# A decoder layer with attention, a selective scan and routed adapters: x times sigmoid as one ScalarE function in place of Tanh and a VectorE product

## The chip, the cores and the metric

The kernel runs on one core of one Trainium2 chip, as one launch. The metric is the device time of that launch in microseconds (us); the median of three runs stands for a kernel. Five engines work side by side, each with its own queue in program order: TensorE (PE) for matrix products, VectorE (DVE), ScalarE (ACT), GpSimd (POOL) and SyncE (SP). They meet only at semaphores, and DMA queues move data beside them.

## The reference

Four batches of 512 tokens, width 512, float32. Three blocks, each added to x:

```
x = x + attention(layernorm(x))                 # 16 heads, 2 key/value heads, causal, rotary
x = x + mamba(hidden=ctx, z=layernorm(x))
x = x + ffn(layernorm(x))                       # silu(gate)*up with rank-16 adapters of 8 experts, top 2

mamba:  c  = depthwise causal conv, 4 taps, of (ctx @ in_proj) + conv_b
        u  = silu(c)                            # silu(v) = v * sigmoid(v)
        dt, B, C = split(u @ x_proj);  dt = softplus(dt @ dt_proj + dt_proj_b)
        state = state * exp(dt * A) + dt * u * B      # over 512 steps, 16 states a channel
        y  = sum(state * C) + D * u
        out = y * silu(z)
```

The gate of the convolution is `u = silu(c)`; the gate of z is `y * silu(z)`. The silu of the feed-forward block is not part of the change.

## The kernel before

Work goes batch by batch, with channels or tokens in tiles of 128 partitions (four tiles of 128x512 for every activation). Each engine's program is written out by hand, in the same order of stages. For batch 0 there is a **head**: in-projection, convolution (VectorE), gate, x-projection (TensorE), softplus inputs (ScalarE), and then a polynomial and the scan on VectorE. The **scan** of a batch is 59 pieces of VectorE work (11 for the polynomial, 48 for 16 states) that a fixed table (`PLAN_FIRST`, `PLAN_NEXT`) spreads over slots of the other stages. After the head come the attention projections and 32 attention steps of batch 0.

Then for t = 0, 1, 2 there is a **transition**, the feed-forward stage of batch t, and the attention of batch t+1. The feed-forward stage has 33 evaluations (`evaluate`: ScalarE Silu, then VectorE times `up`), with scan pieces of batch t+1 from the fifth on. Batch 3 has a transition and a feed-forward stage without a next batch beside them.

The transition, in program order. For each of four tiles of tokens i: TensorE projects the attention output (L871), VectorE adds it to x (`first_sum`, L1170) and takes the statistics (`deviation`), GpSimd the power -1/2, VectorE normalizes (`scaled`, L1026) into `hz`, ScalarE gates (`gate_z`, L662) and VectorE multiplies (`gate_y`). `gate_stages` staggers these: at the fourth tile VectorE does its sum and statistics, then `scaled` of tile 2, `gate_y` of tile 1, `scaled` of tile 3, `gate_y` of tile 2, `gate_y` of tile 3. ScalarE does `gate_z` of tiles 0 to 2, then `conv_tap` of one tile (L521, L522: it frees the PSUM bank of that tile of the next in-projection), then `gate_z` of tile 3, then `conv_tap` of the three others. TensorE does three tiles of the next in-projection (`project_in`, L737; the third needs the bank that the first `conv_tap` frees), then the transposes of the gated output (`transpose_gated`, L880) when all four tiles are gated, then the fourth tile. VectorE sums again (`second_sum`, L1189) and normalizes; TensorE transposes, computes the router (L922) and the base product of feed-forward tile 0 (L892, 16 matmuls), while VectorE routes. ScalarE applies Exp to the router's logits (`ffn_masks`, L666), moves masks (L669), does `evaluate(t, 0)`, the convolution's gate of batch t+1 (`conv_gate`), and `split_first`. VectorE does `evaluate(t, 0)`, `activate(t + 1)` and then `mask_low`. TensorE's x-projection `project_x` (L745) waits tile by tile on `u_ready`.

The convolution's weights and bias are halved beforehand (`conv_half`), so `conv_sb` holds c/2, and silu(c) = (tanh(c/2) + 1) * c/2.
Of the kernel before, what the change touches and what calls it, by code (L numbers as in the profile page):

```python
# [7 lines left out]
ALU = mybir.AluOpType  # L8
ACT = mybir.ActivationFunctionType
# [5 lines left out]
NT = L // P  # L15
# [6 lines left out]
JT = DI // P  # L22
# [169 lines left out]
def decoder_layer(nc, x, ctx_t, wq, wk, wv, wo, w_in, w_x, w_dt, w_lora, w_r, b_down, a_down, w_tiles, w_adapt, w_down,  # L192
                  vectors, constants, out, bc_rows):
    with ExitStack() as stack:
        def sb(name, shape, dt=F32):
            return stack.enter_context(nc.sbuf_tensor(name, shape, dt))
# [4 lines left out]
        def sem(name):  # L201
            return stack.enter_context(nc.semaphore(name))
# [39 lines left out]
        hz = r2[:, 0:4, :]  # L242
        silu_z = [r2[:, k, :] for k in (8, 9, 10, 12)]
# [8 lines left out]
        y_sb = sb("y_sb", [P, JT, L])  # L252
# [5 lines left out]
        u_sb, exp_v, relu_v, conv_sb = state[:, 0, :, :], state[:, 1, :, :], decay[:, 0, :, :], decay[:, 1, :, :]  # L258
# [52 lines left out]
        pv_done = sem("pv_done")  # L311
        inv_moved = sem("inv_moved")
        x1_ready = sem("x1_ready")
        tanh_z = sem("tanh_z")
        z_chain = sem("z_chain")
        gated_ready = sem("gated_ready")
        x2_ready = sem("x2_ready")

        tap_ready = sem("tap_ready")
        conv_chain = sem("conv_chain")  # L320
        conv_tanh = sem("conv_tanh")
        u_ready = sem("u_ready")
        xdbl_full = sem("xdbl_full")
        xdt_ready = sem("xdt_ready")
# [187 lines left out]
        def _(act):  # L512
# [13 lines left out]
            def conv_gate(b):  # L526
                for j in range(JT):
                    act.wait_ge(conv_chain, b * 3 * JT + 3 * j + 3)
                    nc.scalar.activation(exp_v[:, j, :], conv_sb[:, j, :], ACT.Tanh).then_inc(conv_tanh, 1)

            def split_first(b):
                act.wait_ge(xdbl_full, b + 1)
# [80 lines left out]
            def attention(b, slots):  # L613
# [43 lines left out]
                for i in range(NT - 1):  # L657
                    gate_z(b, i)

            def gate_z(b, i):  # L660
                act.wait_ge(xn_ready["z"], b * NT + i + 1)
                nc.scalar.activation(silu_z[i], hz[:, i, :], ACT.Tanh, scale=0.5).then_inc(tanh_z, 1)  # L662

            def ffn_masks(t):
                act.wait_ge(router_shift, t + 1)
# [344 lines left out]
        def _(dve):  # L1010
            tt, ts, stt = nc.vector.tensor_tensor, nc.vector.tensor_scalar, nc.vector.scalar_tensor_tensor
# [23 lines left out]
            def convolve(b, tiles):  # L1035

                for j in tiles:
                    bank, count = use(("xin", j), b)
                    dve.wait_ge(tap_ready, b * JT + j + 1)
                    dve.wait_ge(work_free[bank], count + 1)  # L1040
                    for back in range(1, TAPS):
                        tap = conv_half[:, TAPS * j + TAPS - 1 - back:TAPS * j + TAPS - back]
                        stt(conv_sb[:, j, back:L], xin_sb[:, j, 0:L - back], tap, conv_sb[:, j, back:L],
                            ALU.mult, ALU.add).then_inc(conv_chain, 1)
                        dve.wait_ge(conv_chain, (b * JT + j) * 3 + back)

            def activate(b):

                for j in range(JT):
                    dve.wait_ge(conv_tanh, b * JT + j + 1)  # L1050
                    stt(u_sb[:, j, :], exp_v[:, j, :], 1.0, conv_sb[:, j, :], ALU.add, ALU.mult).then_inc(u_ready, 1)

            def scan_piece(b, piece):
                kind, n = piece
                if kind == "poly":

                    if n == 0:
                        dve.wait_ge(softplus_in, b + 1)
                        ts(du_sb[:], exp_v, POLY[-1], None, ALU.mult).then_inc(poly_chain, 1)
                    elif n < NPOLY:  # L1060
                        dve.wait_ge(poly_chain, b * (NPOLY + 2) + n)
                        stt(du_sb[:].rearrange("p j l -> p (j l)"), du_sb[:].rearrange("p j l -> p (j l)"),  # L1062
                            POLY[NPOLY - 1 - n], exp_v.rearrange("p j l -> p (j l)"), ALU.add, ALU.mult)\
                            .then_inc(poly_chain, 1)
                    elif n == NPOLY:
                        dve.wait_ge(poly_chain, b * (NPOLY + 2) + n)
                        tt(dt_sb[:], du_sb[:], relu_v, ALU.add).then_inc(poly_chain, 1)
                    else:
                        dve.wait_ge(poly_chain, b * (NPOLY + 2) + n)
                        tt(du_sb[:], dt_sb[:], u_sb, ALU.mult).then_inc(poly_chain, 1)  # L1070

                        nc.vector.memset(decay[:, :, :, 0:1], 0.0).then_inc(dt_ready, 1)
                    return
                base = b * 3 * NS + 3 * n
                flat = state[:, n % 2, :, :].rearrange("p j l -> p (j l)")
                if kind == "mul":
                    if n == 0:
                        dve.wait_ge(poly_chain, (b + 1) * (NPOLY + 2))
                        dve.wait_ge(y_init, b * JT + JT)
                    elif n >= 2:  # L1080
                        dve.wait_ge(y_added, 16 * (b * NS + n - 1))
                    dve.wait_ge(bc_loaded[n % 2], 16 * (NS // 2) * b + 16 * (n // 2) + 16)
                    row = bc_sb[:, n % 2, 0, :].unsqueeze(1).to_broadcast([P, JT, L])
                    tt(state[:, n % 2, :, :], du_sb[:], row, ALU.mult).then_inc(scan_chain, 1)  # L1084
                elif kind == "run":
                    dve.wait_ge(decay_ready, b * JT * NS + JT * n + JT)
                    dve.wait_ge(dt_ready, b + 1)
                    dve.wait_ge(scan_chain, base + 1)
                    nc.vector.tensor_tensor_scan(flat, decay[:, n % 2, :, :].rearrange("p j l -> p (j l)"), flat, 0.0,  # L1089
                                                 ALU.mult, ALU.add).then_inc(scan_chain, 1)  # L1090
                else:
                    dve.wait_ge(scan_chain, base + 2)
                    row = bc_sb[:, n % 2, 1, :].unsqueeze(1).to_broadcast([P, JT, L])
                    tt(state[:, n % 2, :, :], state[:, n % 2, :, :], row, ALU.mult).then_inc(scan_chain, 1)  # L1094
# [78 lines left out]

            def gate_y(b, j):

                dve.wait_ge(tanh_z, b * NT + j + 1)
                stt(silu_z[j], silu_z[j], 1.0, hz[:, j, :], ALU.add, ALU.mult).then_inc(z_chain, 1)
                if j == 0:
                    dve.wait_ge(y_added, 16 * (b * NS + NS))
                dve.wait_ge(z_chain, b * NT + j + 1)  # L1180
                stt(silu_z[j], y_sb[:, j, :], 0.5, silu_z[j], ALU.mult, ALU.mult).then_inc(gated_ready, 1)

            def second_sum(t):

                for i in range(NT + 1):
                    if i < NT:
                        bank, count = use(("yt", i), t, True)
                        dve.wait_ge(work_full[bank], count + 1)
                        tt(xb[:, i, :], ps_w[:, bank, :], xa[:, i, :], ALU.add).then_inc(work_free[bank], 1)  # L1189
                        dve.wait_ge(work_free[bank], count + 1)  # L1190
                        deviation("ffn", t, xb, i)
                    if i >= 1:
                        scaled("ffn", t, xb, xn, i - 1)

                nc.vector.tensor_copy(scrap[:], vec[0:1, 0:1]).then_inc(x2_ready, 1)
# [86 lines left out]
            ts(decay_rate[:], decay_rate[:], -1.0, None, ALU.mult).then_inc(consts_ready, 1)  # L1282
            dve.wait_ge(conv_halved, 1)
            convolve(0, range(JT))
            activate(0)
            dve.wait_ge(consts_ready, 4)
            dve.wait_ge(loaded["x"], 16)
            normalize("att", 0, xa, xn_att)
# [5 lines left out]
            for t in range(BATCH - 1):  # L1294
                second_sum(t)
                convolve(t + 1, [0])
                route(t)
                convolve(t + 1, range(1, JT))
                evaluate(t, 0)
                activate(t + 1)  # L1300
                mask_low(t)
                for e in range(1, EVALS):
                    evaluate(t, e)
                    if e in NORM_SLOTS:
                        dve.wait_ge(loaded["x"], 16 * t + 32)
                        deviation("att", t + 1, xa, NORM_SLOTS.index(e))
                    for piece in PLAN_NEXT[e]["dve"]:
                        scan_piece(t + 1, piece)
                    if e in NORM_SLOTS:
                        scaled("att", t + 1, xa, xn_att, NORM_SLOTS.index(e))  # L1310
                weigh_down(t)
                for f in range(FT):
                    rotate(t + 1, f)
                    for piece in PLAN_NEXT[DOWN + f]["dve"]:
                        scan_piece(t + 1, piece)
                finish(t)
                attention(t + 1, PLAN_NEXT)
# [104 lines left out]
```

## Time and profile before

| | |
|---|---|
| median of 3 runs | 1612.33 us (1610.44, 1612.33, 1622.39) |
| profiled execution, its time | 1609.58 us |
| its span, first to last instruction | 1607.8 us |
| mean granted TensorE clock | 0.884 |
| PE busy | 1392.1 us (87%) |
| DVE busy | 1129.0 us (70%) |
| ACT busy | 677.2 us (42%), with 56 ACT_TABLE_LOAD |
| POOL busy | 112.0 us (7%) |

A share of busy time is a mean over stages with different limits. 1.8 us of the profiled execution's time lie outside its span. Times in rows are microseconds from the start of the span; "idle before" is how long the engine had nothing to run, with the instruction that ended it.

### The profile page before, as it was taken

The page shows a single profiled execution, that of the slowest core. Times are in us where ns is not written, and L with a number is a line of the kernel's source. Part 1 is how long each engine was busy: PE and PEld are TensorE (multiplying, and loading weights), DVE is VectorE, ACT ScalarE, POOL GpSimd, SP SyncE. Part 2 cuts the span into 40 slices and gives each one's busy share as a digit, 9 for nine tenths or more (in the row PEclk, how much of TensorE's full clock was granted, in tenths as well). Part 3 has the DMA queues.
Part 4 walks back from the last instruction along what each step waited for, and adds up shares of the span by engine and source line. Part 5 has one row for each costly group of instructions (what it writes and reads, how often), then busy time and mean ns, then how long its engine had stood idle before and what let it go on. Part 6 is the DMA issues. An engine that isn't in the chain of part 4 may idle for free.

```text
span 1607.8 us, 16071 instructions
## 1 busy us (share of the span) xinstructions
PE 1392.1 (87%) x5768; PEld 680.2 (42%) x5768; DVE 1129.0 (70%) x1279; ACT 677.2 (42%) x1491; POOL 112.0 (7%) x116
## 2 busy tenths in 40 slices
PE   5756667999998799899999699899989698799999
PEld 2333334444443354434444255444444255454444
DVE  4899997557989775737998866737998967621120
ACT  5155553344543574343552376251562277211110
POOL 0000001000200000000210000100110000100000
PEclk8855558999999699899999678999999869789999
DMA  4166662114667631112766822012566751102113
GB/s 190 40 151 154 141 144 47 41 49 112 169 144 174 166 67 27 40 35 75 181 142 158 197 70 54 27 31 75 144 150 154 168 134 28 27 13 66 49 33 85
DMA packets 53277, 158.80 MB, mean 99 GB/s; under 512 B 5072, under 2 KB 10704, under 8 KB 44752
## 3 DMA queue, kind: packets, MB, share of 16 engines
q0 software_dynamic: 9216, 67.11, 20.3%
q1 hardware_dynamic: 25664, 54.23, 10.2%
q10 hardware_dynamic: 18320, 36.45, 8.5%
q8 instruction: 47, 0.77, 0.2%
q14 instruction: 30, 0.25, 0.0%
HBM read 86.20 MB, written 4.46 MB: 56 GB/s over the span
## 4 chain that ended last, share of the span: by engine, by line
issue 29%; PE 29%; DVE 28%; DMA 6%; ACT 5%; POOL 3%; ACTq 0%; DVEq 0%; POOLq 0%
DVE state L1089 9%; DMA y_sb<-state 6%; PE ps_a L892 5%; PE ps_a L972 4%; DVE state L1084 4%; PE ps_a L818 3%; DVE state L1094 3%; PE ps_w L871 3%; PE ps_a L904 2%; PE ps_b L832 2%; POOL rstd L476 2%; ACT r L624 2%; PE ps_b L912 2%; PE ps_w L780 2%; DVE neg_max L1124 2%
## 5 line engine op out<-in xcount | busy, mean ns | idle before, releaser
L892 PE MATMUL ps_a<-xt,w_sb 128*128 128x512 f32 x704 | 317.5, 605 | 0.0
L1089 DVE TENSOR_TENSOR_SCAN state<-decay,state 128x2048 f32<-128x2048 f32 x64 | 282.8, 4419 | 7.1 <-ACT decay L582 2.9
L1262 DVE TENSOR_TENSOR r<-r,ps_a 128x512 f32<-128x512 f32 x132 | 88.7, 683 | 208.9 <-ACT r L676 208.9
L818 PE MATMUL ps_a<-r 32*128 32x512 f32 (+3 forms) x512 | 140.5, 634 | 83.2 <-ACT r L624 57.8
L892 PEld LDWEIGHTS ps_a<-xt,w_sb 128*128 128x128 f32 x704 | 136.4, 195 | 172.3 <-issue 172.3
L676 ACT ACTIVATE r<-ps_a 128x512 f32<-128x512 f32 x132 | 78.5, 597 | 299.4 <-PE ps_a L904 160.4
L582 ACT ACTIVATE decay<-dt_sb,decay_rate 128x511 f32<-128x511 f32 x256 | 162.9, 711 | 63.2 <-DVE state L1094 31.2
L624 ACT ACTIVATE r<-ps_a,neg_max 128x128 f32<-128x128 f32 (+3 forms) x256 | 133.8, 534 | 117.7 <-DVE neg_max L1124 117.1
L904 PE MATMUL ps_a<-r,wb_sb 128*128 128x512 f32 x352 | 168.4, 601 | 11.1 <-DVE r L1262 8.9
L972 PE MATMUL ps_a<-wd_sb,r 128*128 128x512 f32 x352 | 162.3, 613 | 0.0
L1084 DVE TENSOR_TENSOR state<-du_sb,bc_sb 128x2048 f32<-128x2048 f32 x64 | 146.3, 2287 | 4.5 <-DMA y_sb<-state 4.3
L1094 DVE TENSOR_TENSOR state<-state,bc_sb 128x2048 f32<-128x2048 f32 x64 | 146.0, 2281 | 0.7
L832 PE MATMUL ps_b<-cst,r 128*128 128x128 f32 x640 | 119.6, 329 | 25.4 <-ACT xt L636 16.8
L1124 DVE TENSOR_REDUCE neg_max<-ps_a 128x2 f32<-128x256 f32 (+3 forms) x128 | 104.0, 814 | 21.6 <-PE ps_a L821 20.6
L904 PEld LDWEIGHTS ps_a<-r,wb_sb 128*128 128x128 f32 x352 | 65.4, 191 | 102.4 <-issue 95.7
L486 POOL DMA_DIRECT2D y_sb<-state x64 | 56.1, 877 | 738.7 <-DVE state L1094 654.7
L972 PEld LDWEIGHTS ps_a<-wd_sb,r 128*128 128x128 f32 x352 | 69.8, 199 | 88.0 <-issue 85.4
L832 PEld LDWEIGHTS ps_b<-cst,r 128*128 128x128 f32 x640 | 88.5, 172 | 34.4 <-issue 28.8
L818 PEld LDWEIGHTS ps_a<-r 32*128 32x128 f32 x512 | 50.2, 239 | 119.6 <-ACT r L624 79.6
L476 POOL TENSOR_TENSOR rstd<-var_eps,cst 128x1 f32<-128x1 f32 x48 | 56.0, 1168 | 554.5 <-DVE var_eps L1022 554.5
L912 PE MATMUL ps_b<-r,ad_sb 128*128 128x512 f32 x176 | 87.6, 622 | 1.4 <-DVE r L1262 1.4
L1062 DVE SCALAR_TENSOR_TENSOR du_sb<-du_sb,state 128x2048 f32<-128x2048 f32 x36 | 82.4, 2288 | 0.6
(122 smaller groups left out, 1465.8 us busy)
## 6 DMA issues: line engine op xcount, KB each, us to landing
y_sb<-state POOLq DMA_DIRECT2D x64, 1024.0 KB, 9.7
bc_sb<-bc_rows ACTq DMA_DIRECT2D x64, 512.0 KB, 5.1
w_sb<-in_w_tiles SPq DMA_DIRECT2D x44, 512.0 KB, 3.9
wd_sb<-in_w_down SPq DMA_DIRECT2D x44, 256.0 KB, 3.5
wb_sb<-in_w_adapt SPq DMA_DIRECT2D x44, 128.0 KB, 2.1
xa<-in_x SPq DMA_DIRECT2D x4, 1024.0 KB, 5.1
out_x<-xb SPq DMA_DIRECT2D x16, 256.0 KB, 6.9
xn_att<-in_ctx_t SPq DMA_DIRECT2D x4, 512.0 KB, 6.3
```

Of the source, the lines that this page charges most:

```text
L582: nc.scalar.activation(decay[:, n % 2, j, 1:L], dt_sb[:, j, 1:L], ACT.Exp, scale=decay_rate[:, j, n:n + 1]).then_inc(decay_ready, 1)
L624: nc.scalar.activation(probs[:, (2 * s + k) % 4, 0:(i + 1) * P], score_place(s, k), ACT.Exp, bias=neg_max[:, s % 2, k:k + 1], accum_out=ro ...
L818: nc.tensor.matmul(score_place(s, k), q_t[rows, m, i * P:(i + 1) * P], k_t[rows, 0:width], start=True, stop=False, tile_position=(rows.sta ...
L832: mm = nc.tensor.transpose(ps_b[:, k, kt * P:(kt + 1) * P], probs[:, (2 * s + k) % 4, kt * P:(kt + 1) * P], ident)
L892: mm = nc.tensor.matmul(ps_a[:, 2 * (f % 2) + half, :], w_sb[:, slot, at + k * P:at + (k + 1) * P], xt[:, k, :], start=(k == 0), stop=Fals ...
L904: mm = nc.tensor.matmul(ps_a[:, 2 * (f % 2) + half, :], wb_sb[:, f % 2, at:at + P], low[:, 2 * half + k - 1, :], start=False, stop=(k == 2 ...
L912: mm = nc.tensor.matmul(ps_b[:, k - 1, :], ad_sb[:, f, :], hk[:, (2 * f + k - 1) % 4, :], start=(f == 0), stop=(f == FT - 1), skip_group_c ...
L972: mm = nc.tensor.matmul(ps_a[:, i, :], hb[:, f, i * P:(i + 1) * P], wd_sb[:, f % 2, :], start=(f == 0), stop=False, skip_group_check=True)
L1084: tt(state[:, n % 2, :, :], du_sb[:], row, ALU.mult).then_inc(scan_chain, 1)
L1089: nc.vector.tensor_tensor_scan(flat, decay[:, n % 2, :, :].rearrange("p j l -> p (j l)"), flat, 0.0, ALU.mult, ALU.add).then_inc(scan_chai ...
L1094: tt(state[:, n % 2, :, :], state[:, n % 2, :, :], row, ALU.mult).then_inc(scan_chain, 1)
L1124: nc.vector.tensor_reduce(neg_max[:, s % 2, :], both, AX.X, ALU.max, negate=True)\
```

## The change

The gate of the convolution becomes one ScalarE instruction a tile, Silu with a scale of 2.0 on c/2, which writes `u_sb` itself; `activate`, four VectorE instructions a batch, goes. The gate of z becomes one ScalarE Silu a tile; VectorE's first product in `gate_y` goes (four a batch), and the second loses its factor 0.5. `exp_v` is no longer a scratch of the gate. The piece of the scan that reads `u_sb` on VectorE waits for `u_ready`, since another engine writes it now. Tanh is used nowhere any more.

```diff
             def conv_gate(b):
                 for j in range(JT):
                     act.wait_ge(conv_chain, b * 3 * JT + 3 * j + 3)
-                    nc.scalar.activation(exp_v[:, j, :], conv_sb[:, j, :], ACT.Tanh).then_inc(conv_tanh, 1)
+                    nc.scalar.activation(u_sb[:, j, :], conv_sb[:, j, :], ACT.Silu, scale=2.0).then_inc(u_ready, 1)
...
             def gate_z(b, i):
                 act.wait_ge(xn_ready["z"], b * NT + i + 1)
-                nc.scalar.activation(silu_z[i], hz[:, i, :], ACT.Tanh, scale=0.5).then_inc(tanh_z, 1)
+                nc.scalar.activation(silu_z[i], hz[:, i, :], ACT.Silu).then_inc(z_ready, 1)
...
-            def activate(b):
-
-                for j in range(JT):
-                    dve.wait_ge(conv_tanh, b * JT + j + 1)
-                    stt(u_sb[:, j, :], exp_v[:, j, :], 1.0, conv_sb[:, j, :], ALU.add, ALU.mult).then_inc(u_ready, 1)
...
                         dve.wait_ge(poly_chain, b * (NPOLY + 2) + n)
+                        dve.wait_ge(u_ready, b * JT + JT)
                         tt(du_sb[:], dt_sb[:], u_sb, ALU.mult).then_inc(poly_chain, 1)
...
             def gate_y(b, j):
 
-                dve.wait_ge(tanh_z, b * NT + j + 1)
-                stt(silu_z[j], silu_z[j], 1.0, hz[:, j, :], ALU.add, ALU.mult).then_inc(z_chain, 1)
+                dve.wait_ge(z_ready, b * NT + j + 1)
                 if j == 0:
                     dve.wait_ge(y_added, 16 * (b * NS + NS))
-                dve.wait_ge(z_chain, b * NT + j + 1)
-                stt(silu_z[j], y_sb[:, j, :], 0.5, silu_z[j], ALU.mult, ALU.mult).then_inc(gated_ready, 1)
+                tt(silu_z[j], y_sb[:, j, :], silu_z[j], ALU.mult).then_inc(gated_ready, 1)
...
             convolve(0, range(JT))
-            activate(0)
...
                 evaluate(t, 0)
-                activate(t + 1)
                 mask_low(t)
```

## Rows read from the trace of the kernel before

**Rows 1.** Windows of two stages: length, PE, PEld, DVE, ACT, POOL busy, clock, DMA, GB/s

```profile
251.00:304.00 53.00, 45.67 (x220) 25.42 (x221) 36.67 (x96) 16.08 (x31) 5.80 (x8) 0.88 0.18 48
304.00:452.00 148.00, 140.41 (x335) 61.10 (x333) 109.68 (x95) 72.19 (x103) 14.37 (x9) 1.00 0.38 100
```

**Rows 2.** Groups of instructions: table loads, Silu, and the VectorE product that goes

```profile
L676 ACT ACTIVATE r<-ps_a 128x512 f32<-128x512 f32 x132 | 78.5, 597 | 299.4 <-PE ps_a L904 160.4 <-PE ps_a L892 138.7
...
L676 ACT ACT_TABLE_LOAD x28 | 35.9, 1283 | 0.5
...
L1177 DVE SCALAR_TENSOR_TENSOR r<-r 128x512 f32<-128x512 f32 x16 | 11.0, 685 | 0.0
```

**Rows 3.** Timeline, ACT, first transition; columns: start, length, instruction, idle before

```profile
262.36 0.63 ACT L662 ACTIVATE r<-r 128x512 f32<-128x512 f32 x1 [0.82 <-DVE r L1026]
...
271.87 0.77 ACT L522 ACTIVATE decay<-ps_w,conv_half 128x512 f32<-128x512 f32 x1
...
292.24 0.23 ACT L666 ACTIVATE rt<-rt 128x32 f32<-128x32 f32 x1 [3.68 <-DVE rt L1214]
```

**Rows 4.** Timeline, ACT, softplus of batch 1

```profile
324.24 1.28 ACT L551 ACT_TABLE_LOAD   x1
325.53 0.63 ACT L551 ACTIVATE state<-state 128x512 f32<-128x512 f32 x1
```

**Rows 5.** Timeline, DVE, first transition

```profile
268.50 0.68 DVE L1170 TENSOR_TENSOR xa<-ps_w,xa 128x512 f32<-128x512 f32 x1
...
297.65 7.03 DVE L1043 SCALAR_TENSOR_TENSOR decay<-decay,conv_half 128x511 f32<-128x511 f32 x9
```

**Rows 6.** Timeline, PE, first transition and the x-projection behind it

```profile
261.12 7.13 PE L871 MATMUL ps_w<-wo_sb,r 128*128 128x512 f32 x16
...
272.69 1.98 PE L737 MATMUL ps_w<-xn_att,win_sb 128*128 128x512 f32 x4 [1.00 <-ACT decay L522]
275.31 2.10 PE L880 MATMUL ps_w<-cst,r 128*128 128x128 f32 x12 [0.64 <-DVE r L1181]
...
291.53 8.52 PE L892 MATMUL ps_a<-xt,w_sb 128*128 128x512 f32 x16
...
309.48 3.60 PE L745 MATMUL ps_b<-state,wx_sb 128*128 128x512 f32 x8
```

**Rows 7.** Timeline, ACT and PE, last transition

```profile
1392.58 0.63 ACT L662 ACTIVATE r<-r 128x512 f32<-128x512 f32 x1 [1.15 <-DVE r L1026]
...
1395.25 3.08 PE L880 MATMUL ps_w<-cst,r 128*128 128x128 f32 x12 [7.06 <-DVE r L1181]
```

**Rows 8.** Timeline of the head, all engines

```profile
3.87 1.28 ACT L685 ACT_TABLE_LOAD   x1 [3.87 <-issue]
...
17.26 1.81 ACT L529 ACTIVATE state<-decay 128x512 f32<-128x512 f32 x3
...
20.79 2.50 DVE L1051 SCALAR_TENSOR_TENSOR state<-state,decay 128x512 f32<-128x512 f32 x4
...
21.63 5.20 PE L745 MATMUL ps_b<-state,wx_sb 128*128 128x512 f32 x8 [5.96 <-DVE state L1051]
...
30.35 0.67 ACT L548 ACTIVATE state<-ps_w,vec 128x512 f32<-128x512 f32 x1
...
38.28 1.23 DVE L1059 TENSOR_SCALAR du_sb<-state 128x2048 f32<-128x2048 f32 x1 [8.95 <-ACT scrap_a L557]
```

**Rows 9.** Timeline, DVE, the fourth sum of the other three transitions

```profile
640.71 0.68 DVE L1170 TENSOR_TENSOR xa<-ps_w,xa 128x512 f32<-128x512 f32 x1
...
1015.95 0.68 DVE L1170 TENSOR_TENSOR xa<-ps_w,xa 128x512 f32<-128x512 f32 x1
...
1388.44 0.68 DVE L1170 TENSOR_TENSOR xa<-ps_w,xa 128x512 f32<-128x512 f32 x1
```

**Rows 10.** Second transition: PE timeline of the base product, and a window (PE busy, clock)

```profile
663.79 10.11 PE L892 MATMUL ps_a<-xt,w_sb 128*128 128x512 f32 x16
...
663.80:674.00 10.20, 10.20 (x20) 0.70 0.00 1
```

More of the change, by code:

```diff
@@ L313, in decoder_layer @@
         x1_ready = sem("x1_ready")
-        tanh_z = sem("tanh_z")
-        z_chain = sem("z_chain")
+        z_ready = sem("z_ready")
         gated_ready = sem("gated_ready")
@@ L320, in decoder_layer @@
         conv_chain = sem("conv_chain")
-        conv_tanh = sem("conv_tanh")
         u_ready = sem("u_ready")
```

## The prediction, made before the change was built

> **What bounds the kernel now.** I read the windows by stage first, then the chain that ended last in the four transitions and the head, and then the timelines of ACT, DVE and PE there, since the change touches no other place. In a feed-forward stage PE is busy for 140.4 of 148 us: PE sets the pace, and DVE work taken out there buys nothing [rows 1]. In a transition no engine is full (PE 45.7, DVE 36.7, ACT 16.1 of 53 us): the tiles pass from engine to engine, and the chain runs through DVE from the last attention projection to the transposes L880 [rows 1, 6]. In the head the chain runs from the convolution through one Tanh, one DVE product, the x-projection and softplus to the first polynomial piece, for which DVE waits 8.95 us; from there DVE is the bound [rows 8]. So a microsecond saved in the head or in a transition is kept, as the next stage simply starts earlier; one saved inside a stage is not. The reader is to see two places of DVE work (four instructions in each transition, four in the head) and one place where ACT gains table loads.
>
 Silu in place of Tanh adds: in the head one before the convolution's gate and one before softplus's Exp; in each of four transitions one before `gate_z` of tile 0 and one before the router's Exp. The load before `evaluate(t, 0)` is there already, and the convolution's gate of batches 1 to 3 comes right after Silu: none. In all 2 + 4 x 2 = 10, 66 instead of 56. By their own rows they take 10 x 1.283 = 12.8 us of ACT. Where they fall: a load goes to the engine before the wait of the activation that needs it (the first is at 3.87, before the activation that then waits for its DMA) [rows 8]. `gate_z` of tile 0 starts at 262.36 after 0.82 us of idling [rows 3]; with the load begun in that gap it starts about 0.5 later, at 262.8, and its result is not used before 267, when `gate_y` comes: nothing. The router's Exp at 292.24 had 3.68 us of idling before it [rows 3], which hides 1.28 whole. Were the load after the wait instead, the router's masks would be ready 1.3 later: DVE ends routing at 297.65 [rows 5], PE takes the masks up only after the base product, at 291.53 + 8.52 = 300.05 [rows 6], so 2.4 us of cover are left. Eight loads at nothing either way.
>
> A load costs its row and no more: it begins at 324.24, ends at 325.52, and Exp starts at 325.53 [rows 4]. The Trainium skill says otherwise ("ScalarE: Activation LUTs", What ACT_TABLE_LOAD costs): some 1283 ns for the load and a drain of about 1380 ns beside it, 2.66 us for each switch; the same page's rule is to group calls by set, which speaks against this change. By an estimate from that page's figure the sum below would shrink to some 3 us; the 1.283 agrees with the trace, the drain is not to be seen in these rows.
>
> **Part 2, the gate of z.** Removed: four DVE products of 0.685 us in each transition [rows 2]. The Silu itself: no row shows it from SBUF. With PSUM input it takes 0.597 [rows 2], Tanh here 0.63 [rows 3]; I take 0.63, the shape and the memory being the same, and 0.03 either way is nothing. Product for product, the remaining one is taken to cost what it costs now. What lies on the path, first transition: PE delivers the fourth projection at 261.12 + 7.13 = 268.25 [rows 6], but DVE, still in `gate_y` of tile 0, takes it at 268.50 [rows 5]: 0.2 saved there. Behind it stand three products more, 3 x 0.70 with the gap, so DVE by itself would be 2.3 ahead. Now the waits. In the last transition ACT has nothing between: `scaled` of tile 3 is ready 0.9 earlier, so `gate_z` of tile 3 starts at 1392.58 - 0.9 = 1391.7 and ends at 1392.3 [rows 7]; DVE arrives at 1392.2 and gains 2.15 instead of 2.3. PE was waiting for just that (7.06 us idle, ended by L1181) [rows 7]: **2.15 us gained**. In the three others `conv_tap` lies on ACT between the gates of tiles 2 and 3: it ends at 271.87 + 0.77 = 272.64 [rows 3], 0.2 earlier with the tiles before it, so the gate of tile 3 runs 272.44 to 273.07 and DVE's product ends at 273.8, 1.5 earlier than now. But PE is in the third tile of the in-projection, which begins when that `conv_tap` frees its bank, at 272.69 - 0.2, for 1.98 us: it is free for the transposes at 274.5, not at 275.31 [rows 6]. What is late next is thus PE and the bank. **0.8 us gained** in each, 2.4 for three. Were PE not in the way it would be 1.5 each, and without `conv_tap` 2.15. After the transposes the old sequence of DVE, PE and ACT follows, shifted whole.
>
> **Part 3, the gate of the convolution.** Batches 1 to 3: four DVE products go, 2.5 us as in the head [rows 8]. What waits for them is `project_x`, and on PE that follows the adapters' product in order: it begins at 309.48 with no idle time before it [rows 6], since u was there already; `mask_low`, behind them on DVE, waits for the same product of PE. So nothing; the cover is PE's, and if it were gone, up to 2.5 us a batch would be won. Head: the load follows the last setup activation, now at about 17.3, where the first three Tanh stood [rows 8]; Silu of tiles 0 to 2 then runs 18.6 to 20.5, and tile 3 when the convolution ends, at 20.79 to 21.42. PE can start at 19.35 instead of 21.63 and needs its 5.20 us for the x-projection [rows 8] (tile 3 is there in time), so it ends at 24.6: 2.25 earlier. Softplus's first activation, at 30.35 now [rows 8], comes at 28.1; then the load of 1.28 stands before Exp, which leaves 0.97. **1.0 us gained**. If the chip's clock treats the start at 19.35 otherwise, the 5.20 could be the 3.60 that the same product takes in batch 1 [rows 6], and 1.6 more is won: up to 2.6. If nothing of the overlap came about, the load would cost 1.3 net: that is the lower bound.
>
> **The wait added** for `u_ready` on DVE stands before a scan piece that comes after softplus, long after u: nothing, and nobody waits behind it. SP's and POOL's queues and all DMAs keep their order.
>
> **The sum:** 1.0 + 3 x 0.8 + 2.15 = 5.55 us. From the profiled execution: 1609.58 - 5.55 = 1604.0. The median shown lies 2.75 above that execution, the lowest run 0.9; I put the median at 1606. That is 0.35%, well below the 1% that a measurement of this kernel can tell from no change.
>
> **The rivals.**
> 1. *The clock falls on the other side (slower).* The transitions are not equal: the fourth sums stand at 268.50, 640.71, 1015.95 and 1388.44, so the cycles take 372.2, 375.2 and 372.5 us [rows 5, 9]. The middle one is longer by 3.0 with the same instructions, and 1.6 of it is seen in the base product, 10.11 for 8.52 us, at a granted clock of 0.70, so partly at the lower level of 1.2 GHz [rows 6, 10]. When the clock rises there is not tied to the program alone, and every stage will now start some microseconds earlier. If both short cycles became long (2 x 3.0) and the last base product too (1.6), 7.6 us would go against 5.55: 1609.58 + 2.05 = 1611.6, median 1614. It decides from two more long cycles on; one alone gives 1607 (median 1609.5). For it: one of three cycles was long. Against: the pauses of PE ahead of it change by under 1 us.
> 2. *The clock falls kindly.* The long cycle becomes short: 1604.0 - 3.0 = 1601.0, median 1603.5. As likely as one more long one.
> 3. *A load holds ACT for longer than its row.* With twice the row, 2.57, the head's Silu begins at 19.9, the x-projection ends at 25.9 (0.95 earlier) and Exp is late by 2.57 - 0.95 = 1.6 instead of early by 1.0; `gate_z` of tile 0 would end at 264.7, still before 267, and the router's 3.68 us still cover it. The sum is 5.55 - 2.6 = 2.95: 1606.6, median 1609. Rows 4 speak against it. This is what the skill's page on ScalarE, as named above, would make of it.
> 4. *PE is not in the way.* If the transposes could start when the gate is done, 1.0 + 3 x 1.5 + 2.15 = 7.65: 1602, median 1604.7. Against: PE's order is fixed, and the in-projection stands ahead.
> 5. *The build puts the tables otherwise*, with a load inside a stage at each decay. No function there changes, so it has next to no chance.
>
> **How the numbers follow.** Forecast 0.50; rival 1 with two or more long cycles 0.05, with one 0.13; rival 2 0.12; rival 3 0.08; rival 4 0.08; the rest, with no gain that stays, 0.04. The eight in ten reach from rival 2 with a little of rival 4 (1601) to one long cycle and the 10 us scatter of the three runs shown, of which the lowest two are 1.9 apart (1612). No case reaches 16 us: faster by over 1% 0.04 and slower by over 1% 0.03, for chips that differ; within 1% 0.93.
>
> **What would show it.** ACT_TABLE_LOAD x66; ACT busy up by about 12.8 us; DVE busy down by 32 x 0.685 = 21.9. L1051 and L1177 gone. L745 in the head begins near 19.3 and the first polynomial piece near 37.3 (step right) or at 39 or later (rival 3). In the first three transitions L880 starts right after L737, with no wait for DVE; in the last it waits for DVE 2.15 less. The distance from the fourth sum to the base product shrinks by 0.6 and, in the last, by 2. The prediction is wrong if a load is seen with its idle gap on the path before the router or the gate of tile 1, or if the cycles stretch inside the feed-forward or attention stages by more than the 3.0 seen now.

## The result and the profile after

The changed kernel takes 1597.83 us (median of 10 runs, 1593.24 to 1608.63) against 1612.61 for the kernel before (10 runs, 1610.44 to 1622.39): a ratio of 0.9904 (95% interval 0.9881 to 0.9926). Timed again beside later experiments it took 1597.07 (ratio 0.9891, 0.9866 to 0.9915). The forecast was 1606 in a range of 1601 to 1612; the gain is 14.8 us where 5.5 were worked out. The profiled execution took 1596.27 us, span 1594.5, mean granted TensorE clock 0.888 (1 is the full clock).

First the page of the changed kernel: busy time of each engine.

```profile
PE 1382.6 (87%) x5768; PEld 675.0 (42%) x5768; DVE 1108.9 (70%) x1247; ACT 689.2 (43%) x1501; POOL 112.0 (7%) x116
```

Work moved as forecast: DVE has 32 instructions fewer and 20.1 us less, ACT ten more and 12.0 more (21.9 and 12.8 in the forecast, which adds up lengths; busy time counts overlaps once). But PE, which the change does not touch and which has its 5768 records as before, is busy for 9.5 us less. That is the line that the forecast has no term for. (xN in a row of PE counts records of the trace: a float32 product of the source leaves two, a transpose one. The router's 16 products are x32, the 8 of a base product x16.)

The table loads of the changed kernel, by line:

```profile
L674 ACT ACT_TABLE_LOAD x28 | 35.9, 1283 | 0.5
...
L580 ACT ACT_TABLE_LOAD x21 | 26.9, 1283 | 25.4 <-DVE state L1087 25.4
...
L549 ACT ACT_TABLE_LOAD x7 | 9.0, 1283 | 0.1
...
L660 ACT ACT_TABLE_LOAD x4 | 5.1, 1283 | 0.1
L664 ACT ACT_TABLE_LOAD x4 | 5.1, 1283 | 0.1
...
L683 ACT ACT_TABLE_LOAD x1 | 1.3, 1283 | 3.7 <-issue 3.7
L527 ACT ACT_TABLE_LOAD x1 | 1.3, 1283 | 0.0
```

They are 66: one more at softplus (L549), four at `gate_z` (L660), four at the router's Exp (L664), one at the head's gate (L527), where the forecast put them.

Then the first transition, ACT, PE and DVE's fourth sum, which answer to [rows 3], [rows 5] and [rows 6]:

```profile
259.77 1.28 ACT L660 ACT_TABLE_LOAD   x1
261.07 0.63 ACT L660 ACTIVATE r<-r 128x512 f32<-128x512 f32 x1
...
269.89 0.77 ACT L520 ACTIVATE decay<-ps_w,conv_half 128x512 f32<-128x512 f32 x1
270.55 0.63 ACT L660 ACTIVATE r<-r 128x512 f32<-128x512 f32 x1
...
285.35 1.28 ACT L664 ACT_TABLE_LOAD   x1
288.73 0.23 ACT L664 ACTIVATE rt<-rt 128x32 f32<-128x32 f32 x1 [2.10 <-DVE rt L1205]
```

```profile
259.34 7.13 PE L869 MATMUL ps_w<-wo_sb,r 128*128 128x512 f32 x16
...
270.71 1.98 PE L735 MATMUL ps_w<-xn_att,win_sb 128*128 128x512 f32 x4 [0.80 <-ACT decay L520]
272.53 0.60 PE L878 MATMUL ps_w<-cst,r 128*128 128x128 f32 x4
...
278.02 3.19 PE L735 MATMUL ps_w<-xn_att,win_sb 128*128 128x512 f32 x4 [1.67 <-DVE xb L1180]
```

```profile
266.51 0.69 DVE L1163 TENSOR_TENSOR xa<-ps_w,xa 128x512 f32<-128x512 f32 x1 [0.51 <-PE ps_w L869]
```

Both loads lie in idle time: Exp still waits 2.10 us for VectorE after its load. The transposes (L878) follow the in-projection's third tile with no wait for DVE: PE and the bank are late next, as the forecast said. The fourth sum now waits for PE (0.51 us) and starts 0.04 us after the projection's end at 266.47; before, it started 0.25 after. In the last transition the transposes wait 4.87 us for DVE instead of 7.06 [rows 7]:

```profile
1383.81 3.08 PE L878 MATMUL ps_w<-cst,r 128*128 128x128 f32 x12 [4.87 <-DVE r L1172]
...
1395.57 6.83 PE L920 MATMUL ps_b<-wr_sb,xt 128*128 128x8 f32 x32
...
1395.60:1402.30 6.70, 6.70 (x34) 0.50 0.01 2
```

The base product of the second transition, which took 10.11 us at a clock of 0.70 [rows 10], and its window here:

```profile
657.83 8.63 PE L890 MATMUL ps_a<-xt,w_sb 128*128 128x512 f32 x16
...
657.80:666.30 8.50, 8.50 (x18) 0.82 0.00 1
```

The same sixteen records are 1.5 us shorter at a higher granted clock (0.82 against 0.70). A stretch at the lower of the clock's two levels is called a low stretch below. The head, ACT, PE and DVE, which answers to [rows 8]:

```profile
16.20 1.28 ACT L527 ACT_TABLE_LOAD   x1
17.50 1.67 ACT L527 ACTIVATE state<-decay 128x512 f32<-128x512 f32 x3
...
27.16 0.67 ACT L546 ACTIVATE state<-ps_w,vec 128x512 f32<-128x512 f32 x1
27.84 1.28 ACT L549 ACT_TABLE_LOAD   x1
...
18.27 5.37 PE L743 MATMUL ps_b<-state,wx_sb 128*128 128x512 f32 x8 [3.79 <-ACT state L527]
...
36.37 1.23 DVE L1051 TENSOR_SCALAR du_sb<-state 128x2048 f32<-128x2048 f32 x1 [9.96 <-ACT scrap_a L555]
```

**Where the time went.** I laid both timelines beside each other at the same instructions and took the distances. "Gates" is from the fourth sum (L1170, now L1163) to the first second sum (L1189, now L1180); "router" from there to the router's first reduction; "base" from there to ScalarE's move after the x-projection; the last feed-forward stage runs from the first masked adapters to the end of the last sum. Times in us, summed over the three transitions where there are three. The columns are single profiles: the kernel before, the same once more, the same with two unread matmuls put in (experiment 8), and the changed kernel three times. Left out are three pieces: from the head to the fourth sum of the first transition (230.2 to 230.7 in all six), the last router part (17.4 in all six), and the way from there to the masked adapters (16.4, 16.5, 16.5, 15.9, 16.0, 17.1).

| stage | before | again | before_fill2 | after | again | timed |
|---|---|---|---|---|---|---|
| head | 38.3 | 38.1 | 37.6 | 36.4 | 38.5 | 36.8 |
| gates, first three | 22.7 | 22.7 | 22.7 | 20.1 | 20.1 | 20.1 |
| router, first three | 47.3 | 47.3 | 46.9 | 46.0 | 45.4 | 45.2 |
| base, first three | 65.6 | 67.1 | 67.5 | 64.7 | 63.2 | 63.2 |
| feed-forward, first three | 676.8 | 677.8 | 678.2 | 676.0 | 676.5 | 676.0 |
| attention of batches 1 to 3 | 307.5 | 314.7 | 307.7 | 305.6 | 307.0 | 305.5 |
| gate, last | 8.0 | 8.0 | 8.0 | 6.0 | 6.1 | 6.0 |
| last feed-forward stage | 175.1 | 175.3 | 173.4 | 173.7 | 173.4 | 175.1 |

The gates repeat to a tenth: 2.55 + 1.98 = 4.5 us, and they are what the change touches. Counted from the end of PE's fourth projection instead of from the fourth sum they are 0.2 us more in each transition: 1.06 us in each of the first three (7.75, 7.82, 7.82 to 6.69, 6.76, 6.76) and 2.19 in the last (8.28 to 6.09), 5.4 us together, alike in all three profiles of the changed kernel. In the table these 0.2 us lie in the stages that end with the fourth sum. The stages below the gates have no instruction more or less on PE, yet they differ by steps of 0.7 to 7 us from one execution to the next, within one kernel, and on the whole lie lower after the change.

How they differ can be read from PE's busy time in the same stretches of the first profile of each kernel: in the routers 34.7 us before and 33.6 after, in the base products 64.1 and 63.2, in the attention of batches 1 to 3 282.2 and 279.5, from the last router to the end 186.6 and 184.7. That is 6.6 us less for stretches that are together 6.0 shorter. PE's idle time there stays within 0.8 us in each, so what got shorter are the matmuls themselves. In the feed-forward stages PE's busy time falls by 3.1 and the stage by 0.8.

### The profile page after: what moved, and what is told of

The parts are those of the page before. It is cut to its first block, busy times and chain, and to the rows that moved or that the text cites. A ratio compares the mean times of both kernels' runs of the same rounds, so it can differ in the third digit from the quotient of the medians.

```text
span 1594.5 us, 16051 instructions
## 1 busy us (share of the span) xinstructions
PE 1382.6 (87%) x5768; PEld 675.0 (42%) x5768; DVE 1108.9 (70%) x1247; ACT 689.2 (43%) x1501; POOL 112.0 (7%) x116
## 3 DMA queue, kind: packets, MB, share of 16 engines
q1 hardware_dynamic: 25664, 54.23, 10.1%
HBM read 86.20 MB, written 4.46 MB: 57 GB/s over the span
## 4 chain that ended last, share of the span: by engine, by line
issue 30%; PE 29%; DVE 26%; DMA 7%; ACT 5%; POOL 2%; ACTq 0%; DVEq 0%; POOLq 0%
DVE state L1082 10%; DMA y_sb<-state 7%; PE ps_a L890 5%; PE ps_a L970 4%; DVE state L1077 4%; PE ps_w L869 3%; DVE state L1087 3%; PE ps_a L816 3%; PE ps_a L902 2%; PE ps_b L830 2%; ACT r L622 2%; POOL rstd L474 2%; DVE neg_max L1117 2%; PE ps_b L910 2%; PE ps_w L778 2%
## 5 line engine op out<-in xcount | busy, mean ns | idle before, releaser
L580 ACT ACTIVATE decay<-dt_sb,decay_rate 128x511 f32<-128x511 f32 x256 | 163.0, 712 | 63.2 <-DVE state L1087 31.2
```

Of the source, the lines that this page charges most:

```text
L580: nc.scalar.activation(decay[:, n % 2, j, 1:L], dt_sb[:, j, 1:L], ACT.Exp, scale=decay_rate[:, j, n:n + 1]).then_inc(decay_ready, 1)
```

## The experiments

Each kernel is timed beside the kernel before on the same chip; every ratio is against it. The names of the two theories: A, the rest of the gain is TensorE's granted clock, which falls otherwise on stages that start otherwise; B, it is work.

**1. The gate of z alone** (z_only): the diff without its parts in `conv_gate`, `activate` and the scan.

> Only the gate of z as changed (Silu on ScalarE, one VectorE product a tile); the convolution's gate stays Tanh and product. Read from the two traces, the four gates of z give 3 x 0.85 + 1.98 = 4.5 us where they lie. Theory A (the rest of the 13.3 us comes from the granted TensorE clock, which falls otherwise on the stages once they start at other times): 4.5 us less than before with several us either way, and every low stretch of the clock that goes or comes beside matmuls shows as a step in the distance between stages. Theory B (the rest is work: VectorE products that are gone also speed up the feed-forward and attention stages): the rest divides among the two parts by their products, so about 4.5 + half of 7 = 8 less, and no step lies where the clock differs.

1606.46 us, ratio 0.9959 (0.9936 to 0.9982): 6.3 us less by the medians. The gates took 6.7, 6.7, 6.7 and 5.6 us. Its attention of batch 1 had a step of 7.6 us, as "before, again" has. Counted from the projection's end its gates gain 5.8 us. The interval reaches from 2.9 to 10.3 us less, so it holds what theory A expected (4.5) and what theory B did (8).

**2. The gate of the convolution alone** (conv_only): the diff's parts in `conv_gate`, `activate` and the scan.

> Only the gate of the convolution as changed (Silu with scale 2.0, no activate on VectorE, two more table loads in the head). Direct gain read from the traces: the head, 1.9 us, of which 0.5 is an input transfer that landed earlier in one profile, so 1.4. Theory A: 1.4 us less, give or take several us of clock. Theory B: 1.4 and the other half of the unexplained 7 us, 5 us less; both parts then add to the 13 to 15 us of the whole change.

1611.51 us, ratio 0.9984 (0.9961 to 1.0008): 1.2 us by the medians, not to be told from nothing. Gates unchanged (7.5, 7.6, 7.6, 8.0). So by the medians the two parts alone, 6.3 and 1.2, do not add to the 14.8 of the whole. The median is against theory B's forecast for this part, 5 us, but the interval reaches 6.3 us less and does not exclude it.

**3. A shift of 1.4 us** (before_d2):

```diff
                         dve.wait_ge(softplus_in, b + 1)
+                        if first_batch(b):
+                            for k in range(2):
+                                tt(dt_sb[:, k, :], cos_t, sin_t, ALU.mult)
```

> The kernel before, with two VectorE products of 128x512 (0.69 us each, their result is overwritten unread) put in ahead of the first polynomial piece of batch 0, on the path. Nothing else changes. Theory B: the time grows by 1.4 us, since all the rest is the same work 1.4 us later. Theory A: the change of the total is not 1.4 but can be anything from -5 to +6, since the stages meet the clock's steps 1.4 us later; the distances between the fourth sums (372.2, 375.2, 372.5 before) change with it.

1614.20 us, ratio 0.9998 (0.9975 to 1.0021). By the medians 1.5 us more, and the profile is the one of before, all marks 1.3 to 1.7 later (span 1609.2). The large jump that theory A allowed did not come: the clock's steps went along with the program. This one shift does not make the difference, which speaks against rival 1's picture of stages sliding past steps of the clock; no other shift was tried.

**4. All ten loads, most of the saving of z put back** (after_zpad):

```diff
                 dve.wait_ge(z_ready, b * NT + j + 1)
+                tt(hz[:, j, :], cos_t, sin_t, ALU.mult)
```

> The changed kernel with a VectorE product of the same size (unread, over hz) put back into each gate of z ahead of the real one: all ten table loads are there, the gate of z saves nothing on VectorE. My forecast's price for the loads (nothing in the transitions): each gate takes as long as before, the transitions' 4.5 us are lost again, and the time is the changed kernel's plus 4.5 by theory B with no clock effect. Theory A: plus 4.5 give or take several us. If instead the loads cost something, the fourth sum to the transposes is longer than before's 6.8 us.

1605.09 us, ratio 0.9947 (0.9924 to 0.9970), 7 us above the changed kernel (each against the kernel before timed beside it), not 4.5. The gates took 7.1, 7.2, 7.2 and 7.7: no longer than before with the loads in, even 0.4 shorter, because the unread product does not depend on its neighbour and follows it sooner (0.60 us from start to start in the rows, 0.71 to 0.78 before). The loads cost nothing there. Against the changed kernel the gates are 3.1 us longer, and the time 7: here too more came than the work itself.

**5. Matmuls in the last pause** (after_warm, before_warm); the results of the matmuls are not read, and `warm(n)` is n products of the source, 2n records:

```diff
+            def warm(n):
+                for _ in range(n):
+                    nc.tensor.matmul(ps_a[:, 3, :], wq_sb[:, 0, 0:P], wo_sb[:, 0, :], start=True, stop=True)
...
+            warm(10)
             transpose_gated(BATCH - 1)
+            warm(4)
             ffn_head(BATCH - 1)
```

> The changed kernel with 14 unread matmuls of 128x512 into a PSUM bank that is free there: 10 in the pause of TensorE before the last transition's transposes (4.9 us in the changed kernel), 4 after them. The router's 32 small matmuls took 6.83 us in the last transition and 3.64 in the first, at the low and the high level of the granted clock, with equal instructions. Theory A (the pause lowers the clock and the low clock lies on the path): the last router product and the transposes beside it speed up, and the time falls by 3 to 5 us. Theory B (no clock on the path): the added matmuls are in a pause and the time stays, or grows by up to 2 us where they get in the way.

> The kernel before with the same 14 unread matmuls in the last transition, where TensorE's pause is 7.1 us. If the gain of the change beyond its 6.4 us of direct savings sits in the last transition and the stage after it (the step of the granted clock at 1434 us is in the profiles of the four kernels with the long pause and in neither of the two with the short one), this kernel gains more than the changed one does by its matmuls, 5 to 7 us, and the difference of the two kernels shrinks. If not, both gain alike.

after_warm: 1597.62, ratio 0.9908 (0.9890 to 0.9926), as the changed kernel. Its last router part fell from 17.4 to 14.0 us, and the gate rose from 6.0 to 9.1: ten matmuls overran the pause by just what the clock gave back. before_warm: 1608.53, ratio 0.9980 (0.9966 to 0.9994), 3 to 4 us less: 17.4 to 13.8 at the router, 8.0 to 8.9 at the gate, while its last feed-forward stage stayed at the longer time. So the low clock of that transition lies on the path and costs 3.4 to 3.6 us, in both kernels alike; it is not where the change found its gain.

**6. Both kernels once more** (before_again, after_again; one profile each, in the table above).

> The kernel before once more, for a second profile. Theory A: the distances between stages change from one execution to the next by steps of 1.4 to 3.4 us that lie where the low stretches of the clock lie; theory B: they repeat within some tenths, as the instructions do.

> The changed kernel once more, for a second profile. The same question as for the kernel before. The direct gains must repeat: fourth sum to first sum of the second kind 0.85 us shorter than before in three transitions and 2.0 in the last; what the rest does need not.

1619.69 and 1598.21 us. before_again is 10.1 us longer in its span than the first profile: 7.2 of it in the attention of batch 1, 1.5 in each of two base parts, of which the third wins 1.6 back, 1.0 in the feed-forward stages. A step of that size in that attention is in the profiles of before_fill (7.2) and z_only (7.6) too. A window of 20 us in that attention, first of before, then of before_again:

```profile
583.00:603.00 20.00, 18.19 (x207) 0.91 0.27 54
```

```profile
586.00:606.00 20.00, 18.71 (x148) 0.63 0.27 54
```

PE is busy for as long, at a clock of 0.63 instead of 0.91, and does 148 records of matmuls instead of 207 in that time. That such steps happen within one kernel, at the place of the low clock, is theory A's point; theory B has nothing that explains them.

**7. The gate of z in the last batch alone** (z_last):

```diff
-                nc.scalar.activation(silu_z[i], hz[:, i, :], ACT.Tanh, scale=0.5).then_inc(tanh_z, 1)
+                if b == BATCH - 1:
+                    nc.scalar.activation(silu_z[i], hz[:, i, :], ACT.Silu).then_inc(tanh_z, 1)
+                else:
+                    nc.scalar.activation(silu_z[i], hz[:, i, :], ACT.Tanh, scale=0.5).then_inc(tanh_z, 1)
...
+                    tt(silu_z[j], y_sb[:, j, :], silu_z[j], ALU.mult).then_inc(gated_ready, 1)
```

> The kernel before with the gate of z changed in the last batch only (two more table loads, four VectorE products fewer). Direct: 2.0 us between the fourth sum and the second sums (8.0 to 6.0). Theory A (a shorter pause of TensorE also moves the granted clock in the stages behind it): the last feed-forward stage falls with it, from 133.2 to 131.5 us, as in all kernels with the short gate, and the whole gains about 4 us. Theory B: 2.0 and no more.

1607.82 us, ratio 0.9979 (0.9961 to 0.9997); its span is 4.4 us below that of before. The gate 8.0 to 5.7, the way from the router to the masked adapters 16.4 to 15.9, the last feed-forward stage 1.6 shorter. The first adapter product of that stage is the same four records behind the same pause of 2.25 us in both. First z_last, with its window:

```profile
1431.61 1.96 PE L907 MATMUL ps_a<-r,wb_sb 128*128 128x512 f32 x4 [2.25 <-DVE r L1269]
...
1431.60:1435.00 3.40, 3.39 (x8) 1.00 0.00 0
```

Then the kernel before, with its window:

```profile
1434.46 3.63 PE L904 MATMUL ps_a<-r,wb_sb 128*128 128x512 f32 x4 [2.25 <-DVE r L1262]
...
1434.50:1438.00 3.50, 3.50 (x5) 0.52 0.00 0
```

**8. The pause ahead of the last feed-forward stage filled** (before_fill with `warm(5)`, before_fill2 with `warm(2)`, before `pe.wait_ge(low_ready, 4 * t + 4)` of the last batch):

> The kernel before with five unread matmuls of 128x512 ahead of the first adapter product of the last feed-forward stage, where TensorE idles 2.25 us and the granted clock falls right behind, in all six profiles with the long gate of z and in none of the four with the short one. Theory A (that low stretch, set off by that pause, is the 1.7 us by which the last stage is longer): it goes, the stage takes 131.5 instead of 133.2, and the whole is 1 to 2 us shorter. Theory B (the stage is longer for another reason): the stage stays at 133.2.

> The kernel before with two unread matmuls, 1.8 us at the high clock, in TensorE's pause of 2.25 us ahead of the last feed-forward stage's first adapter product. Five overran it by 2.2 us. Theory A (the pause sets off the low stretch, which lies on the path): the stage takes 131.5 us instead of 133.2 and the first adapter product 1.9 instead of 3.6. Theory B: 133.2 and 3.6.

before_fill: 1612.68, ratio 0.9996 (0.9978 to 1.0014). The low stretch was gone, but the five matmuls took 4.46 us for a pause of 2.25, and what the clock gave went into the late start: by itself this run decides nothing. before_fill2: 1611.16, ratio 0.9983 (0.9967 to 1.0000), and the row of it:

```profile
1435.03 1.88 PE L877 MATMUL ps_a<-wo_sb,wq_sb 128*128 128x512 f32 x4
1437.44 1.96 PE L908 MATMUL ps_a<-r,wb_sb 128*128 128x512 f32 x4 [0.53 <-DVE r L1268]
```

1.96 instead of 3.63, and the stage 1.7 us shorter. With the pause partly filled that low stretch does not come, and it costs 1.7. Over the profiles without a filler at this place it is there in all six with the long gate of z and in two of the eight with a short one (after_timed, after_warm5).

**9. The improved forms** (after_warm5: five matmuls in place of ten; after_warm_all: three more behind `transpose_gated(t)` of the first three transitions; after_timed: the changed kernel beside them; after_warm5_fill2: five, four, and two ahead of the last stage).

> The changed kernel with 5 unread matmuls, not 10, in TensorE's last pause before the transposes and 4 behind them. Ten took the transposes' start 3.1 us later and gave 3.4 back at the router, a draw. Five at 0.85 us each fit the pause of 4.9: the router part takes 14.0 instead of 17.4 and the gate stays at 6.0, 3 to 4 us less than the changed kernel, if the pause's clock is what costs there; nothing if the gain of the ten came from the later start itself.

> The same, and three unread matmuls in each of the three other transitions between the gated transposes and the fourth tile of the in-projection, where TensorE idles 1.7 us and the in-projection's last four matmuls then take 3.2 (2.0 at the high clock). If clock is on the path there, 1.2 us in each, 3 to 4 us less than with the five alone; the router part goes from 15.2 to 14.

> The changed kernel, timed again beside the others. If the 14.8 us are the change's and not a chip's, 13 to 16 us less than before; by my forecast's own terms 5.5, by the direct savings 6.4.

> The changed kernel with five matmuls in the last pause before the transposes, four behind them and two ahead of the last feed-forward stage. The five alone gave 3.4 at the gate and router, but in their profile the low stretch ahead of the last stage was back (133.2). If the two costs are separate, this has 14.5 and 131.5: 1 to 2 us less than the five alone, 4 to 5 less than the changed kernel.

after_warm5: 1594.37, ratio 0.9881 (0.9861 to 0.9901); gate 5.6, router 14.5. after_warm_all: 1596.28, 0.9890 (0.9869 to 0.9911): the router parts of the first three sum to 45.2, no less than the changed kernel's 45.2 to 46.0, so nothing came of it. after_timed: 1597.07, 0.9891 (0.9866 to 0.9915); its last stage is the long one, 175.1, although its gate is short. after_warm5_fill2: 1594.10, 0.9873 (0.9849 to 0.9898), with 13.8 at the last router and the short last stage. The last is the fastest kernel measured, 3 us below the changed one timed beside it; the intervals overlap, and it is not to be told from after_warm5. The router's product in the last transition with five matmuls ahead of it, and the window of it (after_warm5), against 6.83 us at 0.50 in the changed kernel:

```profile
1392.59 4.36 PE L924 MATMUL ps_b<-wr_sb,xt 128*128 128x8 f32 x32
...
1392.60:1396.80 4.20, 4.20 (x35) 0.82 0.02 4
```

## Why the prediction was wrong, point by point

- **Ten loads, and where they stand**: right, 66 loads. **At nothing in the transitions**: right; Exp still idles 2.10 us behind its load, and after_zpad has gates no longer than before with all loads in. **A load costs its row and no more**: right. In the head it runs from 27.84 to 29.12 behind an activation that starts at 27.16, and Exp starts at 29.14; rival 3, and with it the Trainium skill's drain of 1380 ns ("ScalarE: Activation LUTs", What ACT_TABLE_LOAD costs), is not seen in these rows.
- **Silu as long as Tanh**: right, 0.630 us by row.
- **The gate of z, 0.8 in three transitions and 2.15 in the last**: right in mechanism. The forecast counts from PE's fourth projection, and so counted it is 1.06 and 2.19. `conv_tap`, the bank and PE limit the three as worked out; rival 4, with 1.5 each, is out. The 0.8 took the third tile's row of 1.98 us as what has to pass before the transposes, but they start 1.82 after its start (270.71 to 272.53).
- **The head, 1.0**: roughly right. From DVE's first convolution product to the first polynomial piece it was 26.9 us before and 25.5 after, 1.4; of the other 0.5 of the profile's 1.9, 0.3 came from the context that landed earlier and the rest from the in-projection's first tile. The 1.4 holds where the x-projection takes 5.37 us, as in four of the nine profiles with this head; in four it took 6.3 to 6.5, and in one 3.67, close to the 3.60 that the forecast named as its upper case. So the head scatters: its first polynomial piece stands at 37.6 to 39.3 us in the profiles with the old head and no shift, at 35.6 to 39.1 in those with the new one. Counted from the first convolution product, the mean of nine profiles with the new head is 1.0 us below that of eight with the old one (26.2 to 27.2, before_d2 without its 1.4), and the convolution's part alone gave 1.2 by the medians.
- **The convolution's gate in batches 1 to 3, nothing**: right as far as shown; conv_only has no gain beyond the head's.
- **"After the transposes the old sequence of DVE, PE and ACT follows, shifted whole"**: this is the step that failed. It puts every stage behind the gates at nothing. The direct terms of the first two profiles are 1.4 + 3 x 1.06 + 2.19 = 6.8, against 5.55 in the sum; the other half of the gain, 6.5 us by the first two profiles and 8.0 by the medians, lies in stages that I took as unchanged. Between these two profiles 1.3 are in the routers, 0.9 in the base products, 0.8 and 1.9 in the feed-forward and attention stages (0.6 of the 1.9 is the fourth sum, counted above), 0.4 on the way to the masked adapters, 1.4 in the last stage, 0.5 in the head. Outside the head their matmuls are the same in number and form and are shorter, at a higher granted clock: 0.8865 on average over 15 runs of the changed kernel, 0.8806 over 91 of the one before. The forecast's own sign for this step was that the way from the fourth sum to the base product shrinks by 0.6 us in the first transition; it shrank by 1.5 (23.0 to 21.5).
- **Rival 1 and rival 2** named that clock, but as luck, with a worse case likelier than it deserved. Both pictured stages sliding past steps of the clock. before_d2 slid them by 1.4 us and nothing changed. At the one place that was taken apart, the clock follows what PE does and leaves undone before it: in z_last one shorter gate takes away a low stretch that stands 39 us behind the start of the transposes, and in before_fill2 filling most of the 2.25 us pause in front of it does too. I had priced this at 3.0 for one cycle against the change; it went for the change, in nearly every stage.

**What stays open.** That a shorter gate keeps the clock up later is shown for one place only, and not always: after_timed has the short gate and the long last stage. The parts alone gave 6.3 and 1.2 by the medians, and the whole 14.8; the intervals reach 3.7 us to either side for each part, so much of that may be scatter; if anything is left, it is an interplay that no run here took apart. And the mean clock tells only part of it: runs of the two kernels with a mean clock of 0.884 to 0.889 still differ by 12.1 us (26 runs, mean 1609.5, and 11 runs, mean 1597.4). The runs allow an estimate, with the time at the low level worked out from each run's mean clock (the lower level is half of the higher): within the kernel before (91 runs) a run with 1 us more at the low level is 0.25 us longer (0.27 in the 15 runs of the changed kernel), and the changed kernel has 22 us less at the low level on average. That is worth 5.6 us of the 14.6 between the two means; 9.0 are left, of which 6.8 are the direct terms. By this estimate the last 2.2 us have no cause shown.

## What to carry to other kernels

Sum the direct savings by where they lie, but where TensorE works around pauses (here of one to seven microseconds), give a term to the granted clock: look in the profile for the same group of matmuls with two durations (here 8.5 and 10.1, 1.96 and 3.63, 3.6 and 6.8 us), and ask whether the change makes the pause ahead of it shorter or longer. A function table that has to be changed costs 1.28 us of ScalarE's own time and nothing more where ScalarE idles; taking a VectorE step out of a chain is worth that step only up to what stands next, here a PSUM bank and TensorE's own order. Before crediting a part of a change, run the unchanged kernel twice more with a profile: here one execution of it differed from another by 10 us in stages nobody had touched.

## What the runs showed of the hardware

- Two to ten unread matmuls in a pause kept the granted clock up behind it: the router's 16 small products (32 records) took 4.36 us instead of 6.83, and two products (four records) 1.96 instead of 3.63. Filling more than the pause takes back what it gives (4.46 us of filler in a pause of 2.25; ten matmuls in one of 4.9 took the gate from 6.0 to 9.1).
- More time at the low level in an attention stage cost 7.2 us in one of two profiles of the same kernel, with the same instructions around it (clock 0.63 against 0.91 over 20 us).
- A table load starts ahead of its activation's wait: at 285.35, right behind the last move; it ends at 286.63, and only 2.10 us later has VectorE the router's logits ready.
